# Counting edges in ranges of 16 nodes for three tiles (was 32 for six), with the lower parts of the turned inputs made from PSUM

## The reference

```python
# layer 0: GCN with self loops, batch norm, gelu, residual
xw  = x @ W.T
deg = segment_sum(1, col);  norm = rsqrt(deg[row]) * rsqrt(deg[col])
h   = segment_sum(norm[:, None] * xw[row], col) + b
x   = layernorm(x + gelu(batch_norm(h)) + x)
# layer 1: two gated relational layers
def rgcn(x, basis, att, gate_w, root, bias):
    w = einsum('rb,bio->rio', att, basis)          # basis: 30 x 512 x 512
    msg[e] = (sigmoid(x[col[e]] @ gate_w[type[e]]) * x[col[e]]) @ w[type[e]]
    return segment_sum(msg, row) + x @ root + bias
h = relu(rgcn(x, basis1, ...));  x = layernorm(x + rgcn(h, basis2, ...))
```

## Time and profile before

| | |
|---|---|
| median of 3 runs | 328.7 us (328.42 to 328.86) |
| the profiled execution | 328.01 us, of which the span is 326.2 us |
| PE busy | 291.7 us, 89% |
| DVE busy | 179.9 us, 55% |
| ACT busy | 140.9 us, 43% |
| POOL busy | 48.1 us, 15% |
| moved by DMA | 73.66 MB, 226 GB/s over the span |

### The profile page before, as it was taken

The page is one execution under the profiler, slowest core; times in us unless marked ns, Lnnn a source line. Parts: engine busy times, 40 slices in busy tenths (PEclk is TensorE's granted clock), DMA queues, the critical chain, the costliest instruction groups (busy, mean ns, idle before and its releaser), DMA issues.

```text
span 326.2 us, 4834 instructions
## 1 busy us (share of the span) xinstructions
PE 291.7 (89%) x1709; PEld 198.1 (61%) x1709; DVE 179.9 (55%) x502; ACT 140.9 (43%) x274; POOL 48.1 (15%) x80
## 2 busy tenths in 40 slices
PE   0778999997898999647999999999997999999991
PEld 0644656643336668414686655657796877787771
DVE  3789987999979755688401024035246125433333
ACT  5499997989710458748225213220412242100000
POOL 2334400000000920372000000000001900010000
PEclk9999999999796799969999999999999999999997
DMA  6972888599797799909999578979000510001112
GB/s 174 341 318 96 332 330 291 245 395 420 293 393 304 257 317 409 401 36 335 418 353 406 194 280 337 378 280 363 13 0 0 132 31 0 2 0 32 31 33 63
DMA packets 12757, 73.66 MB, mean 226 GB/s; under 512 B 1952, under 2 KB 2195, under 8 KB 4540
## 3 DMA queue, kind: packets, MB, share of 16 engines
q1 hardware_dynamic: 11282, 70.82, 57.1%
q0 software_dynamic: 1104, 2.36, 2.9%
q10 hardware_dynamic: 346, 0.17, 0.2%
HBM read 72.05 MB, written 1.28 MB: 225 GB/s over the span
## 4 chain that ended last, share of the span: by engine, by line
PE 69%; DVE 16%; DMA 5%; issue 5%; ACT 1%; POOL 1%; DVEq 1%; SPq 0%; POOLq 0%
PE psW L490 13%; PE psM L471 11%; PE psM L473 10%; PE psM L472 10%; PE psM L712 7%; PE psM L732 6%; PE psE L566 5%; DVE oh_key L1050 4%; PE psM L618 3%; DMA basis_ring<-in_L_gnn_basis_dram 3%; DMA xs<-in_x_dram 3%; DVE w L1033 1%; DVE B L1040 1%; DVE x_sum L1167 1%; DVE AT L1100 1%
## 5 line engine op out<-in xcount | busy, mean ns | idle before, releaser
L490 PE MATMUL psW<-basis_ring,S 128*32 128x512 f32 x512 | 65.9, 634 | 1.0 <-DMA basis_ring<-in_L_gnn_basis_dram 1.0
L1050 DVE TENSOR_SCALAR oh_key<-iota_f,key 128x320 f16<-128x320 f16 x162 | 46.8, 330 | 4.9 <-DVE B L1040 1.7
L1214 DVE SCALAR_TENSOR_TENSOR zg<-psM,gate,zg 125x512 fp32r<-125x512 f32 x20 | 15.0, 751 | 57.9 <-ACT zg L904 57.9
L566 PE MATMUL psE<-oh_key,oh_src 128*125 128x320 f16 x162 | 35.6, 340 | 5.5 <-DVEq L1042 3.7
L566 PEld LDWEIGHTS psE<-oh_key,oh_src 128*125 128x125 f16 x162 | 21.9, 145 | 25.2 <-issue 13.9
L780 ACT ACTIVATE oh_diff<-iota_f,edgeT 128x128 f16<-128x128 f16 x108 | 34.3, 389 | 1.5 <-ACT xT_full L794 0.8
L904 ACT ACTIVATE zg<-psM,gate 125x512 fp32r<-125x512 f32 x20 | 13.8, 689 | 46.1 <-PE psM L473 45.7
L471 PE MATMUL psM<-w,hlT 128*125 128x512 f32 x80 | 32.4, 405 | 0.1
L490 PEld LDWEIGHTS psW<-basis_ring,S 128*32 128x32 f32 x512 | 13.7, 113 | 29.8 <-issue 26.1
L473 PE MATMUL psM<-w,hlT 128*125 128x512 f32 x80 | 31.6, 395 | 0.0
L472 PE MATMUL psM<-w,hlT 128*125 128x512 f32 x80 | 31.6, 395 | 0.0
(11 more groups left out here) (161 smaller groups left out, 451.3 us busy)
## 6 DMA issues: line engine op xcount, KB each, us to landing
basis_ring<-in_L_gnn_basis_dram SPq DMA_DIRECT2D x64, 1024.0 KB, 6.8
root_raw<-in_L_gnn_root_dram POOLq DMA_DIRECT2D x32, 64.0 KB, 3.5
xs<-in_x_dram SPq DMA_DIRECT2D x1, 1120.0 KB
out_dram<-xs SPq DMA_DIRECT2D x5, 224.0 KB
w_raw<-in_L_gnn_W_dram SPq DMA_DIRECT2D x1, 1024.0 KB, 10.4
bias_b<-in_L_gnn_bias_dram POOLq DMA_DIRECT2D x1, 250.0 KB, 3.3
xs<-in_x_dram SPq DMA_DIRECT2D x1, 130.0 KB
out_dram<-xs SPq DMA_DIRECT2D x5, 26.0 KB
```

The lines of the kernel that those rows point to most:

```text
L490: m = nc.tensor.matmul(psW[32 * j:32 * j + 32, cc % 2, :], S[:, cc % 2, cc // CH, q].rearrange("p k r -> p (k r)"), ring[:, n % RING, j, : ...
L566: nc.tensor.matmul(psE[0:PC, g % 2, 0:KEYS], oh_src[:, g % 3, j * P:j * P + PC], oh_key[:, t % OH, :], start=(j == 0), stop=(j == G - 1)). ...
L1050: v.tensor_scalar(oh_key[:, t % OH, :], iota_f[:, 0:KEYS], key[:, t:t + 1], None, ALU.is_equal) \
L1214: link(v.scalar_tensor_tensor(out=zg[:, 1, c, r, :], in0=bank(("Z", L, c, r))[0:PC, :], scalar=gate[:, L, c, r:r + 1], in1=zg[:, 0, c, r, ...
```

## The change

- A range is now three tiles and 16 destinations (`SG = 3`, `W = 16`): KEYS is 160, `oh_key` and the moving side of the counting matmuls are half as wide, and there are NW = 54 ranges. Within three tiles `dst` spans at most 13. A group is still six tiles and one `psE` bank; the bank holds two ranges side by side.
- `add_window` runs 54 times, each 125 x 160, after the second and the fourth tile of a group. It no longer waits for its own result (`link`); the next one waits for it instead, so VectorE makes one-hots in between.
- The least and greatest destination are taken for each half row (`mm` is 81 x 2 x 2, four small transposes instead of two), `base` is 54 wide.
- GpSimd's nine subtractions and ScalarE's nine `..._full` copies are gone. ScalarE makes hi from PSUM (`turned_high`), and VectorE makes lo from PSUM and hi (`turned_low`), nine times, after groups 1 to 5.
- TensorE: `base` and `att` go before the first turns, three turns stand before group 0, and the others after groups 0 to 3 (`TURN_AT`).
- The five small instructions that count further rounds (`rounds`) move on VectorE from group 1 to group 12.

```diff
-W = 32
+SG = 3
+NW = T // SG
+W = 16
-        for name in turned[0:2]:
-            use(name, "act")
-        use("base", "dve")
         use("att", "dve")
-        for name in turned[2:]:
-            use(name, "act")
+        for name in turned:
+            use(name, "dve")
-        FIRST_TURNS = 4
+        FIRST_TURNS = 3
+        TURN_AT = {0: (3,), 1: (4, 5), 2: (6, 7), 3: (8,)}
+        TURNED_LOW_AT = {1: (0, 1), 2: (2, 3), 3: (4, 5), 4: (6, 7), 5: (8,)}
+        ROUNDS_AT = 12
...
-                nc.gpsimd.tensor_tensor(lo, full, hi.bitcast(F32), ALU.subtract).then_inc(in_lo, 1)
...
                 if g >= 2:
-                    pe.wait_ge(win_added, g - 1)
+                    pe.wait_ge(win_added, 2 * (g - 1))
                 for j in range(G):
                     t = g * G + j
                     pe.wait_ge(key_ready, t + 1)
-                    nc.tensor.matmul(psE[0:PC, g % 2, 0:KEYS], oh_src[:, g % 3, j * P:j * P + PC],
-                                     oh_key[:, t % OH, :], start=(j == 0), stop=(j == G - 1)).then_inc(adj_used, 1)
-                if g + FIRST_TURNS < len(turned):
-                    turn(g + FIRST_TURNS)
+                    at = j // SG * KEYS
+                    nc.tensor.matmul(psE[0:PC, g % 2, at:at + KEYS], oh_src[:, g % 3, j * P:j * P + PC],
+                                     oh_key[:, t % OH, :], start=(j % SG == 0), stop=(j % SG == SG - 1)) \
+                        .then_inc(adj_used, 1)
+                for i in TURN_AT.get(g, ()):
+                    turn(i)
...
+            def turned_high(i):
+                wait_full(act, turned[i])
+                hi, _, ps = turned_parts(i)
+                nc.scalar.activation(hi, ps, ACT.Copy).then_inc(in_hi, 1)
...
+            def turned_low(i):
+
+                dve.wait_ge(in_hi, i + 1)
+                hi, lo, ps = turned_parts(i)
+                link(v.tensor_tensor(lo, ps, hi.bitcast(F32), ALU.subtract))
+                dve.sem_inc(free_dve, 1)
+                dve.sem_inc(in_lo, 1)
...
-            def add_window(g):
-
-                at = nc.values_load(base_i[0:1, g:g + 1], engines=[mybir.EngineType.DVE], min_val=0, max_val=N - 1)
-                dve.wait_ge(adj_used, min(T, G * (g + 1)))
+            def add_window(w):
+
+                g, h = w // 2, w % 2
+                at = nc.values_load(base_i[0:1, w:w + 1], engines=[mybir.EngineType.DVE], min_val=0, max_val=N - 1)
+                if h == 0:
+                    dve.wait_ge(adj_used, G * (g + 1))
+                if w:
+                    dve.wait_ge(win_added, w)
                 to = B[:, :, :, bass.ds(at, W)]
-                link(v.tensor_tensor(to, to, psE[0:PC, g % 2, 0:NC * WIN].rearrange("p (c t w) -> p c t w", c=NC, t=R),
-                                     ALU.add))
-                dve.sem_inc(win_added, 1)
+                v.tensor_tensor(to, to, psE[0:PC, g % 2, h * KEYS:(h + 1) * KEYS]
+                                .rearrange("p (c t w) -> p c t w", c=NC, t=R), ALU.add).then_inc(win_added, 1)
...
-                if t == 2 * G - 1:
+                if t == G - 1:
+                    v.tensor_copy(base_i[:], gmm[0:1, 0, :])
                     build_S()
-                    rounds()
-                    dve.wait_ge(b_zero, 1)
-                if t % G == 1 and t > 2 * G:
-                    add_window(t // G - 2)
+                    dve.wait_ge(b_zero, 1)
+                if t % G == G - 1:
+                    for i in TURNED_LOW_AT.get(t // G, ()):
+                        turned_low(i)
+                if t == ROUNDS_AT * G:
+                    rounds()
+                if t % G in (1, 3) and t > 2 * G:
+                    add_window(t // SG - 4)
```

More of the change, by code:

```diff
@@ L59 @@
 V_GATE, V_BIAS1, V_B, V_GAMMA, V_BETA, NV = 0, 2 * R, 2 * R + 1, 2 * R + 2, 2 * R + 3, 2 * R + 4
-assert T == NG * G and T == 2 * ROWS and G % 2 == 0
+assert T == NG * G and T == 2 * ROWS and G == 2 * SG
 KB = 16
@@ L335, in own, with turned_parts @@
             return BG * q - bases(q).start
+        def turned_parts(i):
+            what, c = turned[i]
+            n = slice(c * PC, (c + 1) * PC)
+            if what == "xT":
+                return xT_hi[:, :, n], xT_lo[:, :, n], bank(turned[i])[:, 0:KC * PC].rearrange("p (k n) -> p k n", k=KC)
+            return w0T_hi[:, c, :], w0T_lo[:, c, :], bank(turned[i])
         def w_block(L, kc):
@@ L512, in _ @@
             pe.wait_ge(minmax_ready, 1)
-            for i in range(2):
-                last[0] = nc.tensor.transpose(bank("minmax")[0:1, i * ROWS:(i + 1) * ROWS], mm[:, i:i + 1],
+            for i, h in itertools.product(range(2), range(2)):
+                last[0] = nc.tensor.transpose(bank("minmax")[0:1, i * T + h:(i + 1) * T:2], mm[:, i, h:h + 1],
                                               ident[0:ROWS, 0:ROWS])
@@ L541, in xw_part @@
                     done()
-            for i in range(2):
-                turn(i)
             pe.wait_ge(base_ready, 1)
             wait_free(pe, "base")
-            last[0] = nc.tensor.matmul(bank("base")[:, 0:NG], ones_f[0:1, :], gmm[0:1, 0, :], start=True, stop=True)
+            last[0] = nc.tensor.matmul(bank("base")[:, 0:NW], ones_f[0:1, :], gmm[0:1, 0, :], start=True, stop=True)
             done()
@@ L556, in _ @@
             done()
-            for i in range(2, FIRST_TURNS):
+            for i in range(FIRST_TURNS):
                 turn(i)
@@ L826, in _ @@
                     release(nc.scalar.activation(xw[:, c, :], bank(("xw", c))[0:PC, :], ACT.Copy), ("xw", c), "act")
-                if g + 2 < len(turned):
-                    turned_parts(g + 2)
+                for i in TURNED_LOW_AT.get(g, ()):
+                    turned_high(i)
             w_first(2)
@@ L950, in _ @@
             for i, op in enumerate((ALU.min, ALU.max)):
-                last = v.tensor_reduce(mm[:, i:i + 1], rows_f[:, 1].rearrange("t h e -> t (h e)"), AX.X, op)
+                last = v.tensor_reduce(mm[:, i, :], rows_f[:, 1], AX.X, op)
             last.then_inc(minmax_ready, 1)
@@ L980, in _ @@
             wait_full(dve, "base")
-            link(v.tensor_copy(base_b[:], bank("base")[:, 0:NG]))
+            link(v.tensor_copy(base_b[:], bank("base")[:, 0:NW]))
             dve.sem_inc(free_dve, 1)
-            link(v.tensor_tensor(key2[:].rearrange("p (g t) -> p g t", t=G),
-                                 edgeT[:, 1, :].rearrange("p (g t) -> p g t", t=G),
-                                 base_b[:].unsqueeze(2).broadcast_to([P, NG, G]), ALU.subtract))
+            link(v.tensor_tensor(key2[:].rearrange("p (g t) -> p g t", t=SG),
+                                 edgeT[:, 1, :].rearrange("p (g t) -> p g t", t=SG),
+                                 base_b[:].unsqueeze(2).broadcast_to([P, NW, SG]), ALU.subtract))
             link(v.tensor_scalar(key[:], key2[:], float(W), 1000.0, ALU.is_ge, ALU.mult))
@@ L1061, in _ @@
                     w_low(LOW_AT[t // G])
-            add_window(NG - 2)
-            add_window(NG - 1)
+            for w in range(NW - 4, NW):
+                add_window(w)
+            dve.wait_ge(win_added, NW)
             more = nc.values_load(more_i[0:1, 0:1], engines=[mybir.EngineType.DVE], min_val=0, max_val=N // W)
```

43 lines of the change are left out of this document (9 added, 34 removed).

## The result

| | before | after |
|---|---|---|
| median | 328.9 us (20 runs) | 327.14 us (325.26 to 330.67, 20 runs) |
| ratio, 95% interval | | 0.9948 [0.9924, 0.9972] |
| profiled execution, its span | 328.01, 326.2 us | 326.88, 325.0 us |
| first key of the loop | 16.69 | 13.84 |
| first key of group 14 | 59.93 | 60.59 |

The forecast was 319.7 us with a range of 315 to 324, so the sign was right and the size was not. `AT` was to start 9.0 us earlier and started 2.9 earlier. The loop itself, from its first key to `AT`, takes 81.35 us; before it took 81.37. In these two executions all the time won is won ahead of the loop, and inside it gain and loss cancel.

The account below looks back on a forecast made before the run. Loop bound by VectorE to about 32 us, TensorE to 65.03, then VectorE. Gains of 2.0, 2.7 and 4.8 us, less 0.5 and 0.8, put `AT` 9.0 earlier: 328.01 to 319.0, median 319.7, range 315.0 to 324.0.

Parts of the forecast that it names:

- Costs of the pieces: Steady loop: key 0.17 us, add 0.31 with 0.24 to the next key, six counting matmuls 0.43, a group 1.84.
- Part 1: Up to group 6: VectorE no faster (12.2 us removed, 11.7 added), TensorE ends group 6 at 41.6; gain 2.0 us.
- Part 2, groups 7 to 10: First groups of the TensorE-bound stretch 7 to 13: 0.38 us gained for each group, 2.7 for all seven.
- Part 2, groups 11 to 13: Rest of that stretch: VectorE and ScalarE wait for TensorE, 2.6 us a group on average; TensorE ends group 13 at 60.3.
- Part 3 and tail: Groups 14 to 26, VectorE bound: 4.8 us more gained, 0.5 given back for waits; tail adds 0.8, `AT` at 89.1.
- all three meet: Last part of the loop: VectorE, ScalarE and the weight ring finish together near 85 us; 0.5 us given back.
- Behind the loop: After `AT`: order and sizes stay the same and the ring's rhythm moves with `AT`, so nothing differs.
- More in the early part: Rival, up to group 6: loads covered and lower parts 0.67 us without wait gain 3 us more, 316.5 us; chance 0.18.
- The loads are not covered: Rival, second add of each group: register loads show, 3.3 us a group (345; 0.04) or mildly 2.1 (322.5; 0.13).
- TensorE's clock: Rival, last part: TensorE at 1.2 GHz, 324.5 us, chance 0.12; granted clock 0.5 within 60 to 87 us would show error.
- No change: Rival, behind the loop: time saved is given back because the ring is empty when the loop ends earlier; 328.7 us, chance 0.03.
- the hard form: Rival, second add of each group: each register load waits for the add before, 3.3 us a group, about 16 slower; chance 0.04.

Follow-up runs that it names:

- e2: Kernel before (ranges of 32 for six tiles) with only the lower parts moved to VectorE and the new order of turns; 331.7 us, ratio 1.0073.
- e1: Changed kernel with hi and lo parts back on ScalarE and GpSimd and the old order of turns, so only the ranges of 16 are new; 324.3 us, 0.9847.
- e6: Changed kernel with a lower part not waited for at once but released behind the next group's second key; 325.7 us, ratio 0.9913.
- e5: Changed kernel with `rounds` moved from group 12 to group 8 on VectorE; 326.4 us, ratio 0.9923.
- e11: e5 with weight parts 10 and 11 used in group 12 instead of group 13; 324.4 us, ratio 0.9884 of the kernel before.
- e7: e1 with `rounds` in group 8; 323.4 us, ratio 0.9838 of the kernel before.
- e9: e8 with weight parts 10 and 11 used in group 12 instead of group 13; 321.6 us, ratio 0.9785 of the kernel before.
- e8: e7 with `base` ahead of the first two turns on TensorE; 323.1 us, ratio 0.9806 of the kernel before.
- e10: e8 with weight parts 14 to 27 loaded to a quarter of their bytes, the rest left out; 321.5 us, ratio 0.9770 of the kernel before.
- e4: Kernel before with weight parts 10 to 27 loaded to a quarter, the rest left out; 329.9 us, ratio 1.0016.
- e12: Changed kernel with every register load in `add_window` made twice, 54 more; 353.4 us, ratio 1.0753.

## Why the prediction was wrong, step by step

- **Costs of the pieces: right.** Key 0.171 between starts (0.17 forecast), add 0.32 long and 0.24 to the next start (0.31, 0.24), group 1.85 (1.84), six counting matmuls 0.41.
- **Part 1, a gain of 2.0: wrong by all of it.** The terms for the lower parts and the exposed loads were too small. Weights of group 6 end at 43.51, against 43.58 before and 41.6 forecast. Nine lower parts cost 0.91 to 0.93 each with the wait, not 0.82, and the load shows before both adds of a group, 0.6 and not 0.4. Estimated from these, 0.1 x 9 and 0.2 x 5 are 1.9, which is what is missing; e2 against before and after against e1 confirm that the lower parts are what costs (4.4 and 6.1 us up to group 14). e6 took the wait away and got 1.0 of it back; in its rows the load then shows by 0.88 instead of 0.44, which fits that it was not more.
- **Part 2, groups 7 to 10: right.** From 43.52 to 54.90, 11.38 instead of 12.85 (43.58 to 56.43): 0.37 a group, forecast 0.38.
- **Part 2, groups 11 to 13: the step that failed most.** It said that VectorE and ScalarE wait for TensorE, "so no cost shows", from an average of 2.6 us a group. But TensorE's groups are not alike. In the chain of the kernel after, a group with weights takes 3.7 (45.51 to 49.21) and one without 2.0 behind weights (43.52 to 45.51) and 1.8 otherwise (0.41 + 1.43). Groups 11 and 12 have none, so TensorE needs 3.8 for both together, as much as VectorE's 2 x 1.85 or ScalarE's 2 x 1.93, and leaves nothing to hide more work in. VectorE had 2.4 for the merge and 1.1 for `rounds` besides, and 1.5 of register loads in the open, which the prediction had at nothing behind group 6; ScalarE had 2.0 for the upper halves of the weights. Held at 49.46, VectorE took 11.1 us for groups 11 to 13 and came to group 14 at 60.59, where the forecast let it in at 55.2. Of these 5.4 us, 1.9 are from part 1, the other 3.5 arose here. e5 and e11 show the 1.4 of it that hangs on `rounds`; that on the merge wasn't tried.
- **Part 3 and tail: right as a length.** From the first add of group 15 to `AT` the forecast had 30.1 us (59 to 89.1), measured are 30.5 (64.67 to 95.19). The sentence "all three meet" held: VectorE 9.33, ScalarE 9.87 of 10 us and DMA at 1.00 between 70 and 80. Its consequence was not drawn: an earlier VectorE gained nothing (e5, e7) until the ring was asked earlier too (e9, e11).
- **Behind the loop: right but for the clock.** From `AT` to the end of the last weight part 139.03 us before and 139.05 after. From there to the end it is 89.1 before and 90.7 after; the granted clock is 0.83 between 245 and 255 us (1.00 before), which is the lower level for about 3.4 of these 10 us. This 1.6 us is in the profiled executions of after, e1, e8 and e10, but also in that of e4 (90.8), which is the kernel before but for its loads, and in none of the nine others (89.1 to 89.2). So it is no work that was added and not bound to the change. What sets it off is not shown, and whether every execution of after has it isn't either, since one was profiled.
- **The rivals.** "More in the early part" fell: it went the other way. "The loads are not covered" fell for the kernel as built, 1.85 for a steady group against its 3.3 or 2.1; but the cover had nothing to spare (e12, 3.09 with each load twice), and outside the steady part the loads did show. TensorE's clock did fall within 60 to 87 us, which the prediction named as a sign of being wrong (0.97 and 0.69 in the two stretches from 70 to 90), but from group 15 to `AT` only 0.4 us is missing, so it explains little of the loop in after. "No change", by time given back behind the loop, came nearest in its number and fell as a mechanism: the distances behind `AT` didn't grow but for the clock. Some times of rivals don't follow from their own terms: 3 from 319.7 are 316.7 and 322.7, not 316.5 and 322.5, and the hard form's 12.7, 5 and 0.5 give 17 to 18, not 16. None of it bears on the result.

In the sum: of the 9.0 forecast 5.4 were gone when VectorE came to group 14, 0.3 more went within group 14 (60.59 to the add at 64.67 is 4.1, forecast 3.8), 0.4 from there to `AT`. That leaves 2.9 at `AT`, of which 1.6 went to the clock near 250 us, and the span is shorter by 1.2.

## What to carry to other kernels

Where engines take turns as the bound, divide the stretch until each piece has one bound, and never let an average over unlike groups say that another engine is covered; an engine that may be only two groups ahead cannot save up for the group in which it has more to do. Test a wait that looks costly by taking away its cause, and look at what is asked for from a ring by the work that frees its places: moving that work by one group gave 0.9 to 1.5 us from group 14 to `AT` here, after 0.9 to 1.4 us of VectorE's time alone had given none. Time two halves of a change apart, as one of them may pay for the other.

## What the runs showed of the hardware that was not expected

- A register load with its checks takes VectorE's sequencer 0.6 us, and doubling it put 1.24 us on a group of 1.85, so ten short instructions hid two loads and nothing further (e12). The Trainium skill ("DMA: Bandwidth & Descriptors", "Latency and other measured facts") gives a register load a floor of about 600 ns. By the rows the load alone takes 0.30, and only the whole chain comes to 0.6, so the prediction's 0.73 from load to add already held that. What e12 adds is an estimate: since all of the 1.24 showed, a chain longer by 0.3 would not have been hidden either.
- Behind a wait for DMA the same matmuls of one weight part ran at either level, and the length of that wait alone does not tell at which: 1.93 us after 2.45 of waiting (e5 at 78.19) and 1.94 after 1.74 (e1 at 73.95), but 1.06 after 2.30 (after at 77.50) and after 1.20 (e11 at 75.03). In after the granted clock was still 1.00 from 77 to 79 us and 0.50 from 80 to 84.
- While a GpSimd copy of 8 x 512 ran, a pair of VectorE's keys took 1.08 us instead of 0.43, although the copy has only 8 partitions. A lower part, which reads one operand from PSUM, was not stretched by the same copy: 0.69 at 25.25 in e5, with the copy from 24.92 to 25.97. The two rows of after:

```profile
24.62 1.04 POOL L424 COPY vec_rows_q<-vec_rows 8x512 f32<-8x512 f32 x1 [22.17 <-DMA vec_rows<-in_L_gnn_beta_dram]
```

```profile
24.81 1.08 DVE L1047 TENSOR_SCALAR oh_key<-iota_f,key 128x160 f16<-128x160 f16 x2 [0.24 <-DVE w0T_lo L1002]
```
